# Normalising half the tiles of each layer norm on GpSimd instead of all of them on VectorE

## The chip, the cores and the metric

The kernel runs on one core of one Trainium2 chip, in one launch. The metric is the device time of that launch in microseconds (us), taken as the median of several runs; lower is better. The core's engines are TensorE (PE, with its weight loads shown apart as PEld), VectorE (DVE), ScalarE (ACT), GpSimd (POOL) and SyncE (SP, which here only issues DMAs). Each runs its own list of instructions in order, and they wait for one another through semaphores.

## The reference, cut to what matters

The model is a stack of eight residual blocks on an activation of 16 x 256 x 128 float32 values. Every block first normalises its input row by row, without gain or bias:

```python
def _layernorm(x, axis=-1, eps=1e-05):
    m = jnp.mean(x, axis=axis, keepdims=True)
    v = jnp.var(x, axis=axis, keepdims=True)
    return (x - m) / jnp.sqrt(v + eps)
...
x = x + _L0_attn_a_ref(_layernorm(x, axis=-1), ...)
x = x + _L0_ffn_ref(_layernorm(x, axis=-1), ...)
x = x + _L0_attn_b_ref(_layernorm(x, axis=-1), ...)
x = x + _L0_ffn_ref(_layernorm(x, axis=-1), ...)
x = x + _L1_attn_a_ref(_layernorm(x, axis=-1), ...)
x = x + _L1_ffn_ref(_layernorm(x, axis=-1), ...)
x = x + _L1_attn_b_ref(_layernorm(x, axis=-1), ...)
x = x + _L1_ffn_ref(_layernorm(x, axis=-1), ...)
```

So there are eight layer norms (n1 to n8 in the kernel), each over 4096 rows of 128 values. What the blocks compute behind them is not touched.

## The kernel before, in words

The activation lives in the on-chip tile `X` for the whole launch: 128 partitions, 32 tiles of 128 rows, 128 float32 values per row. `XN` holds the normalised rows in the same layout, and `XNT` the same with rows and columns exchanged, which is what the matmuls of the next block read. The program is a chain of phases. Each ends in a clearing of its semaphores and a barrier of all engines (`Phase.__exit__`, lines 81 to 87), so nothing of one phase runs beside another.

`layernorm` (from line 237) is such a phase and is called eight times:

- VectorE takes the statistics of the 32 tiles (`tile_statistics`, L230) and turns them into one mean and one reciprocal deviation per row (`row_statistics`, L208 to L221, with the square root on ScalarE in between, L262).
- VectorE then normalises the 32 tiles one by one (L255), each in one instruction that subtracts the mean and multiplies by the reciprocal deviation. Both are columns of one value per partition. After every fourth tile it raises the semaphore `normed`.
- TensorE waits for `normed`, then turns the four tiles of the group by a multiplication with the identity (L273) into one PSUM bank of four, and raises `turn`.
- ScalarE waits for `turn` and copies the bank of 512 columns to `XNT` (L265), which raises `evac`. TensorE needs `evac` of the group four earlier before it writes to a bank again.

GpSimd has no work in this phase. The loop over the eight groups that sets the order on VectorE is this:

```python
for g in range(G):
    for t in range(4 * g, 4 * g + 4):
        ins = nc.vector.tensor_scalar(sh.XN[:, t, :], sh.X[:, t, :], mean[:, t:t + 1], rstd[:, t:t + 1],
                                      ALU.subtract, ALU.mult)
    ins.then_inc(normed, 1)
```

`row_statistics` is also called by `top2_mixture` (a mixture of experts that ends in a layer norm of its own, twice in the program); there too VectorE alone uses what it returns. Two other places serve the prediction as measurements only: `routing_constants` (L137 to L168), where GpSimd fills tiles while VectorE copies one, and a stage of `delta_attention` (L1963 to L2011) with the same kind of turned tiles.

Of the kernel before, what the change touches and what calls it, by code (L numbers as in the profile page):

```python
# [15 lines left out]
ALU = mybir.AluOpType  # L16
# [17 lines left out]
def reached(eng, sem, count):  # L34

    if not isinstance(count, int) or count > 0:
        eng.wait_ge(sem, count)
# [163 lines left out]
                pool.wait_ge(made, 3)  # L201


def row_statistics(nc, dve, st, mean, rstd, work, chain, sqrt_in, sqrt_done):

    even, odd = (st[:, :, 1], st[:, :, 2]), (st[:, :, 4], st[:, :, 5])
    a, b, c = work[:, 0, :], work[:, 1, :], work[:, 2, :]
    nc.vector.tensor_tensor(a, even[0], odd[0], ALU.add).then_inc(chain, 1)  # L208
    nc.vector.tensor_tensor(b, even[0], odd[0], ALU.subtract).then_inc(chain, 1)
    nc.vector.tensor_tensor(c, even[1], odd[1], ALU.add).then_inc(chain, 1)  # L210
    dve.wait_ge(chain, 3)
    nc.vector.tensor_scalar(mean[:], a, 0.5, None, ALU.mult).then_inc(chain, 1)
    nc.vector.scalar_tensor_tensor(out=work[:, 3, :], in0=b, scalar=0.25, in1=b, op0=ALU.mult,
                                   op1=ALU.mult).then_inc(chain, 1)
    dve.wait_ge(chain, 5)
    nc.vector.scalar_tensor_tensor(out=work[:, 4, :], in0=c, scalar=1.0 / P, in1=work[:, 3, :], op0=ALU.mult,
                                   op1=ALU.add).then_inc(chain, 1)
    dve.wait_ge(chain, 6)
    nc.vector.tensor_scalar(work[:, 5, :], work[:, 4, :], 1e-5, None, ALU.add).then_inc(sqrt_in, 1)
    dve.wait_ge(sqrt_done, 1)  # L220
    nc.vector.reciprocal(rstd[:], work[:, 6, :]).then_inc(chain, 1)  # L221
    dve.wait_ge(chain, 7)


def tile_statistics(nc, dve, st, src, stats):

    with dve.Fori(0, TILES // 8) as m:
        for i in range(8):
            t = 8 * m + i
            nc.vector.bn_stats(st[:, bass.ds(t, 1), :].rearrange("p a s -> p (a s)"),  # L230
                               src[:, bass.ds(t, 1), :].rearrange("p a c -> p (a c)")).then_inc(stats, 1)
    dve.wait_ge(stats, TILES)


def layernorm(nc, sh, name):

    G = TILES // 4
    with Phase(nc, name) as ph:
        st, mean, rstd, work = ph.sb("st", [P, TILES, 6]), ph.sb("mean", [P, TILES]), ph.sb("rstd", [P, TILES]), \
            ph.sb("work", [P, 7, TILES])
        turned = ph.bank("turned", (P, 4, 512))
        stats, chain, sqrt_in, sqrt_done = ph.sem("stats"), ph.sem("chain"), ph.sem("sqrt_in"), ph.sem("sqrt_done")
        normed, turn, evac = ph.sem("normed"), ph.sem("turn"), ph.sem("evac")
        with nc.Block() as block:
            @block.vector
            def _(dve):  # L250
                tile_statistics(nc, dve, st, sh.X, stats)
                row_statistics(nc, dve, st, mean, rstd, work, chain, sqrt_in, sqrt_done)
                for g in range(G):
                    for t in range(4 * g, 4 * g + 4):
                        ins = nc.vector.tensor_scalar(sh.XN[:, t, :], sh.X[:, t, :], mean[:, t:t + 1], rstd[:, t:t + 1],  # L255
                                                      ALU.subtract, ALU.mult)
                    ins.then_inc(normed, 1)

            @block.scalar
            def _(act):  # L260
                act.wait_ge(sqrt_in, 1)
                nc.scalar.activation(work[:, 6, :], work[:, 5, :], ACT.Sqrt).then_inc(sqrt_done, 1)  # L262
                for g in range(G):
                    act.wait_ge(turn, g + 1)
                    nc.scalar.activation(sh.XNT[:, g * 512:(g + 1) * 512], turned[:, g % 4, :], ACT.Copy).then_inc(evac, 1)  # L265

            @block.tensor
            def _(pe):
                for g in range(G):
                    pe.wait_ge(normed, g + 1)  # L270
                    reached(pe, evac, g - 3)
                    for i in range(4):
                        ins = nc.tensor.transpose(turned[:, g % 4, i * P:(i + 1) * P], sh.XN[:, 4 * g + i, :], sh.ident[:])  # L273
                    ins.then_inc(turn, 1)
# [549 lines left out]
def top2_mixture(nc, sh, name, Wg, bg, W1, b1, W2, b2, gamma, beta):  # L824
# [8 lines left out]
    with Phase(nc, name) as ph:  # L833
# [17 lines left out]
             "b2_mm", "b2_ok", "up_mm", "hid_ok", "down_mm", "acc_ok"))  # L851
        st, mean, rstd, work = ph.sb("st", [P, TILES, 6]), ph.sb("mean", [P, TILES]), ph.sb("rstd", [P, TILES]), \
            ph.sb("work", [P, 7, TILES])
        stats, chain2, sqrt_in, sqrt_done, centred, shifted, summed = (ph.sem(x) for x in (
            "stats", "chain2", "sqrt_in", "sqrt_done", "centred", "shifted", "summed"))

        def two_chunks(n, first):

# [2 lines left out]
        with nc.Block() as block:  # L861
            @block.sync
            def _(sp):
                sp.dma_start(wg[:], Wg).then_inc(wl, 16)
                sp.dma_start(bgb[:], bg.partition_broadcast(P)).then_inc(wl, 16)
                sp.dma_start(b2s[:], b2).then_inc(wl, 16)
                sp.dma_start(w1[:], W1.rearrange("e d f -> d e f")).then_inc(loaded, 16)
                sp.dma_start(w2[:], W2.rearrange("e (j f) d -> f e j d", j=2)).then_inc(loaded, 16)
                with nc.allow_non_contiguous_dma("the biases are a few thousand values"):
                    sp.dma_start(b1s[:], b1.rearrange("e (j f) -> f e j", j=2)).then_inc(loaded, 16)  # L870
                sp.dma_start(gam[:], gamma.partition_broadcast(P)).then_inc(loaded, 16)
                sp.dma_start(bet[:], beta.partition_broadcast(P)).then_inc(loaded, 16)
# [162 lines left out]
        with nc.Block() as block:  # L1035
            @block.vector
            def _(dve):
                dve.wait_ge(stats, TILES)
                row_statistics(nc, dve, st, mean, rstd, work, chain2, sqrt_in, sqrt_done)
                with dve.Fori(0, TILES // 8) as m:  # L1040
                    for i in range(8):

                        t = 8 * m + i
                        a, x = (buf[:, bass.ds(t, 1), :].rearrange("p a c -> p (a c)") for buf in (acc, sh.X))
                        nc.vector.scalar_tensor_tensor(out=a, in0=a, scalar=mean[:, bass.ds(t, 1)], in1=gam[:],
                                                       op0=ALU.subtract, op1=ALU.mult).then_inc(centred, 1)
                    for i in range(8):
                        t = 8 * m + i
                        a, x = (buf[:, bass.ds(t, 1), :].rearrange("p a c -> p (a c)") for buf in (acc, sh.X))
                        dve.wait_ge(centred, t + 1)  # L1050
                        nc.vector.scalar_tensor_tensor(out=x, in0=a, scalar=rstd[:, bass.ds(t, 1)], in1=x,
                                                       op0=ALU.mult, op1=ALU.add).then_inc(summed, 1)

            @block.scalar
            def _(act):
                act.wait_ge(sqrt_in, 1)
                nc.scalar.activation(work[:, 6, :], work[:, 5, :], ACT.Sqrt).then_inc(sqrt_done, 1)
# [1191 lines left out]
```

## Time and profile before

| | us |
|---|---|
| median of 3 runs | 4605.37 (4603.25 to 4612.34) |
| the profiled execution | 4600.9 |
| its span in the trace | 4599.1 |
| first normalising instruction to last copy to `XNT`, sum over the eight layer norms | 77.11 |
| VectorE's share of that in L255 | 66.33 |

The 1.8 us between the profiled execution and its span lie outside the traced instructions. Busy time is the time in which an engine ran an instruction, and a share of the whole span is a mean over very different phases, so the layer norms have to be read in windows of their own. The duration of one instruction is longer than the distance from one start to the next on the same engine, as an engine starts the next before the last has quite ended; where instructions follow each other closely, the distance is the price.

### The profile page before, as it was taken

Reading aid. Unit: us, or ns where it says so; the run is one execution under the profiler, and the core shown is the slowest. Engines: PE = TensorE matmul, PEld = TensorE weight load, DVE = VectorE, ACT = ScalarE, POOL = GpSimd, SP = SyncE. Lnnn points to the kernel's source line nnn. Section 1 sums busy time; section 2 is a strip of 40 time slices with the busy share of each in tenths; the row PEclk is TensorE's granted clock in tenths of the full one; section 3 lists DMA queues with packets and bytes.
Section 4 is the critical chain, followed back from the end, with each engine's and each line's share of the span. In section 5 each row is a group of like instructions: output and inputs, shape, how many; then the busy total and the mean of one; then the engine's idle time right before and its main releaser. Section 6 shows DMA issues by size and latency. Waiting matters only on the chain. (4 is left out here: it accounts for less than half of the span.)

```text
span 4599.1 us, 93352 instructions
## 1 busy us (share of the span) xinstructions
PE 3851.2 (84%) x24738; PEld 3022.9 (66%) x24738; DVE 3002.7 (65%) x9151; ACT 2152.0 (47%) x6005; POOL 1073.1 (23%) x2042
## 2 busy tenths in 40 slices
PE   7999999999889699999988968999999386433267
PEld 5888888888767466666656746888888264322145
DVE  5666666666633566666663345999999245899954
ACT  4555555555523344444442324777777133211123
POOL 1222222222200000000000002333333132466633
PEclk9999999999989899999998989999999588766678
DMA  0000000000000000000000000000000411000003
GB/s 23 4 3 1 4 4 3 1 4 4 0 20 0 3 3 2 2 2 2 4 1 20 0 4 5 6 6 6 6 6 5 76 47 37 1 1 1 1 14 87
DMA packets 79403, 48.07 MB, mean 10 GB/s; under 512 B 20928, under 2 KB 73936, under 8 KB 79280
## 3 DMA queue, kind: packets, MB, share of 16 engines
q1 hardware_dynamic: 74736, 37.40, 3.7%
q0 software_dynamic: 4544, 9.35, 0.6%
q8 instruction: 39, 0.64, 0.1%
q14 instruction: 84, 0.69, 0.1%
HBM read 25.94 MB, written 16.59 MB: 9 GB/s over the span
## 5 line engine op out<-in xcount | busy, mean ns | idle before, releaser
L346 POOL TENSOR_TENSOR aa_prob<-aa_prob,aa_inv 128x128 f32<-128x128 f32 (+1 forms) x512 | 248.5, 506 | 919.1 <-DVE aa_inv L562 914.6
L369 PE MATMUL aa_proj<-aa_xs,aa_w 128*128 128x256 f32 x1280 | 362.5, 398 | 12.4 <-DMA aa_w<-in_L_attn_a_W_qkv 10.9
L753 ACT ACTIVATE ab_prob<-ab_ps_score,ab_low 128x128 f32<-128x128 f32 (+1 forms) x512 | 211.0, 422 | 328.4 <-DVE ab_low L786 328.4
L477 ACT ACTIVATE aa_qkv<-aa_proj 128x512 f32<-128x512 f32 x384 | 229.3, 597 | 258.7 <-PE aa_proj L369 198.1
L1712 ACT ACTIVATE lm_prob<-lm_ps_score,lm_low 128x256 f32<-128x256 f32 x512 | 236.7, 471 | 157.2 <-DVE lm_low L1786 85.3
L1662 PEld LDWEIGHTS lm_ps_out<-la_v,lm_probT 128*128 128x128 f32 x2048 | 253.3, 192 | 73.5 <-issue 65.9
L2050 PE MATMUL dr_bank<-da_rT,da_spread 128*128 (+1 forms) x256 | 96.5, 466 | 244.1 <-ACT dr_RW L2068 237.1
L648 POOL COPY ab_xs<-ab_latT 128x256 f32 (+1 forms) x128 | 51.2, 400 | 1032.6 <-PE ab_proj L665 724.7
L1641 PE MATMUL lm_ps_score<-lm_unit 128*128 128x256 f32 x1024 | 270.2, 387 | 5.5 <-DVE lm_unit L1776 5.5
L1662 PE MATMUL lm_ps_out<-la_v,lm_probT 128*128 (+1 forms) x2048 | 257.5, 252 | 19.4 <-issue 16.3
L369 PEld LDWEIGHTS aa_proj<-aa_xs,aa_w 128*128 128x128 f32 x1280 | 214.1, 191 | 44.7 <-issue 12.7
L1604 POOL TENSOR_TENSOR lm_sq<-lm_comp 128x512 f32<-128x512 f32 x128 | 133.4, 1042 | 465.7 <-DVE lm_comp L1753 465.7
L535 DVE SCALAR_TENSOR_TENSOR aa_look<-aa_th_look,aa_ahead 128x384 f32<-128x384 f32 x256 | 183.1, 715 | 88.5 <-ACT aa_th_look L483 88.5
L488 ACT ACTIVATE aa_th_su<-aa_look_su 128x384 f32<-128x384 f32 x256 | 125.5, 490 | 242.8 <-PE aa_look_su L413 242.8
L2100 POOL TENSOR_TENSOR dr_toward<-dr_S,XN 128x64 f32<-128x64 f32 x512 | 181.0, 372 | 217.6 <-DVE dr_S L2129 154.4
L2050 PEld LDWEIGHTS dr_bank<-da_rT,da_spread 128*128 128x128 f32 x256 | 59.2, 238 | 259.4 <-issue 249.5
L494 ACT ACTIVATE aa_prob<-aa_minus,aa_low 128x128 f32<-128x128 f32 (+1 forms) x512 | 225.5, 444 | 0.9 <-DVE aa_low L554 0.9
L1768 DVE RECIPROCAL lm_inv_n<-lm_norm 128x256 f32<-128x256 f32 x128 | 223.1, 1743 | 0.1
L542 DVE SCALAR_TENSOR_TENSOR aa_gated<-aa_th_su,aa_look_su 128x384 f32<-128x384 f32 x256 | 142.0, 555 | 108.5 <-ACT aa_th_su L488 106.9
L273 PE MATMUL n_turned<-ident,XN 128*128 128x128 f32 x256 | 55.7, 370 | 181.7 <-DVE XN L255 181.5
L1776 DVE TENSOR_TENSOR lm_unit<-lm_comp,lm_inv_n 64x512 f32<-64x512 f32 x256 | 201.9, 789 | 7.4
L786 DVE TENSOR_REDUCE ab_low<-ab_ps_score 128x1 f32<-128x128 f32 (+1 forms) x512 | 158.3, 351 | 65.5 <-PE ab_ps_score L677 65.5
(435 smaller groups left out, 10803.4 us busy)
## 6 DMA issues: line engine op xcount, KB each, us to landing
rt_slots<-rc_empty SPq DMA_DIRECT2D x2, 2515.5 KB, 26.2
lm_unit<-la_qk SPq DMA_DIRECT2D x256, 16.0 KB
XN<-rt_back SPq DMA_DIRECT2D x8, 512.0 KB, 6.2
aa_w<-in_L_attn_a_W_qkv SPq DMA_DIRECT2D x8, 384.0 KB, 3.4
out<-X SPq DMA_DIRECT2D x1, 2048.0 KB, 8.7
fc_xin<-rt_slots SPq DMA_DIRECT2D x1, 1483.5 KB, 10.4
fd_xin<-rt_slots SPq DMA_DIRECT2D x1, 1483.5 KB, 10.1
fa_w<-in_L_ffn_W SPq DMA_DIRECT2D x1, 1024.0 KB, 5.4
```

The source lines that it names most:

```text
L346: ins = nc.gpsimd.tensor_tensor(prob[:, h, a:b], prob[:, h, a:b], inv[:, h, t:t + 1].broadcast_to([P, b - a]), ALU.mult)
L369: ins = nc.tensor.matmul(proj[:, i * SEQ:(i + 1) * SEQ], w[:, m, :], xs[:, k, :], start=True, stop=True)
L477: nc.scalar.activation(qkv[:, k, j, :, :].rearrange("p a b -> p (a b)"), proj[:], ACT.Copy, scale=SCALE if j == 0 else 1.0).then_inc(kept, 1)
L494: nc.scalar.activation(prob[:, h, a:b], minus[:, h, a:b], ACT.Exp, bias=low[:, h, t:t + 1], scale=-1.0, accum_out=total[:, h, t:t + 1]).th ...
L535: nc.vector.scalar_tensor_tensor(out=look[:, h, :], in0=th_look[:, h, :], scalar=1.0, in1=ahead[:], op0=ALU.add, op1=ALU.mult).then_inc(lo ...
L753: nc.scalar.activation(prob[:, h, a:b], ps_score[:, h, a:b], ACT.Exp, bias=low[:, h, t:t + 1], accum_out=total[:, h, t:t + 1]).then_inc(ex ...
L1641: ins = nc.tensor.matmul(ps_score[:, h, c * SEQ:(c + 1) * SEQ], unit[:, j, i, h, 0, c, :], unit[:, j, i, h, 1, :, :], start=True, stop=True)
L1662: ins = nc.tensor.matmul(ps_out[:, i, (2 * h + s) * HD:(2 * h + s + 1) * HD], probT[:, h, t, s * P:(s + 1) * P], v[:, bass.ds((n % BATCH) ...
L1712: nc.scalar.activation(prob[:, h, s, :], ps_score[:, h, s * SEQ:(s + 1) * SEQ], ACT.Exp, bias=low[:, h, s:s + 1], accum_out=totals[:, i, h ...
L1768: nc.vector.reciprocal(inv_n[:, j, i], norm[:, j, i]).then_inc(inv_ok, 1)
L1776: ins = nc.vector.tensor_tensor(unit[rows, j, i, h], comp[rows, j, i], inv_n[rows, j, i].unsqueeze(2).broadcast_to([64, 2, 2, HALF]), ALU. ...
L2100: nc.gpsimd.tensor_tensor(toward[:, :, part], S[:, :, part], WV[:, half, :, part, j], ALU.add).then_inc(toward_ok, 1)
```

## The change

In `layernorm`, VectorE now normalises the first two tiles of each group of four and GpSimd the last two, with the same operation and operands. GpSimd starts when VectorE has written the reciprocal deviations, told by a new semaphore `known`, and raises a second new semaphore, `normed_too`, after each pair. TensorE waits for both `normed` and `normed_too` before it turns a group. In `row_statistics` the last step raises `known` instead of the seventh count of `chain`, so `top2_mixture` gets a semaphore of that name as well and is otherwise as before.

```diff
-def row_statistics(nc, dve, st, mean, rstd, work, chain, sqrt_in, sqrt_done):
+def row_statistics(nc, dve, st, mean, rstd, work, chain, sqrt_in, sqrt_done, known):
...
-    nc.vector.reciprocal(rstd[:], work[:, 6, :]).then_inc(chain, 1)
-    dve.wait_ge(chain, 7)
+    nc.vector.reciprocal(rstd[:], work[:, 6, :]).then_inc(known, 1)
+    dve.wait_ge(known, 1)
...
                 for g in range(G):
-                    for t in range(4 * g, 4 * g + 4):
+                    for t in range(4 * g, 4 * g + 2):
                         ins = nc.vector.tensor_scalar(sh.XN[:, t, :], sh.X[:, t, :], mean[:, t:t + 1], rstd[:, t:t + 1],
                                                       ALU.subtract, ALU.mult)
                     ins.then_inc(normed, 1)
+
+            @block.gpsimd
+            def _(pool):
+                pool.wait_ge(known, 1)
+                for g in range(G):
+                    for t in range(4 * g + 2, 4 * g + 4):
+                        ins = nc.gpsimd.tensor_scalar(sh.XN[:, t, :], sh.X[:, t, :], mean[:, t:t + 1], rstd[:, t:t + 1],
+                                                      ALU.subtract, ALU.mult)
+                    ins.then_inc(normed_too, 1)
...
                 for g in range(G):
                     pe.wait_ge(normed, g + 1)
+                    pe.wait_ge(normed_too, g + 1)
                     reached(pe, evac, g - 3)
```

GpSimd's list from the end of the loading phase (L183) through the first layer norm into the first block, before; `ISA` rows are the clearing of semaphores at a phase's end (L86) or, at L346, a setting that stands ahead of GpSimd's first use of a kind of instruction:

```order
L183 UNCONDITIONAL_BRANCH [waits ld_made]
L86 ISA [waits barrier_Pool_Activation_PE_DVE_SP_gather] x2
L324 UNCONDITIONAL_BRANCH [waits barrier_Pool_Activation_PE_DVE_SP_gather]
L326 MEMSET aa_causal 128x384
L327 MEMSET aa_ahead 128x384
L328 MEMSET aa_bar 128x128
```

The same stretch of GpSimd in the changed kernel (its lines below the edit are 11 higher):

```order
L183 UNCONDITIONAL_BRANCH [waits ld_made]
L86 ISA [waits barrier_Pool_Activation_PE_DVE_SP_gather]
L260 UNCONDITIONAL_BRANCH [waits barrier_Pool_Activation_PE_DVE_SP_gather]
L265 ISA
L265 TENSOR_SCALAR XN<-X,n_mean,n_rstd 128x128 [waits n1_known]
L265 TENSOR_SCALAR XN<-X,n_mean,n_rstd 128x128 x15
L249 UNCONDITIONAL_BRANCH
L86 ISA [waits barrier_Pool_Activation_PE_DVE_SP_gather]
L335 UNCONDITIONAL_BRANCH [waits barrier_Pool_Activation_PE_DVE_SP_gather]
L337 MEMSET aa_causal 128x384
L338 MEMSET aa_ahead 128x384
```

Sixteen normalising instructions have come in between the two barriers, with one wait ahead of the first; the setting now stands at L265, ahead of that wait, in the first layer norm alone, and is gone from the first block. The other seven layer norms get the sixteen instructions without it.

TensorE's list at the start of the first layer norm, before:

```order
L267 UNCONDITIONAL_BRANCH [waits barrier_Pool_Activation_PE_DVE_SP_release]
L273 MATMUL n_turned<-ident,XN 128x128 [waits n1_normed]
L273 MATMUL n_turned<-ident,XN 128x128 x3
L273 MATMUL n_turned<-ident,XN 128x128 [waits n1_normed]
L273 MATMUL n_turned<-ident,XN 128x128 x3
```

And in the changed kernel:

```order
L277 UNCONDITIONAL_BRANCH [waits barrier_Pool_Activation_PE_DVE_SP_release]
L284 MATMUL n_turned<-ident,XN 128x128 [waits n1_normed_too,n1_normed]
L284 MATMUL n_turned<-ident,XN 128x128 x3
L284 MATMUL n_turned<-ident,XN 128x128 [waits n1_normed_too,n1_normed]
L284 MATMUL n_turned<-ident,XN 128x128 x3
```

TensorE's instructions stand in the same order; each group's first one has one wait more.

## Rows read from the trace of the kernel before

**Rows 1.** The page: span, and the turning of the layer norms in its costliest groups.

```profile
span 4599.1 us, 93352 instructions
...
L273 PE MATMUL n_turned<-ident,XN 128*128 128x128 f32 x256 | 55.7, 370 | 181.7 <-DVE XN L255 181.5
```

**Rows 2.** Windows, one per layer norm, first L255 to last L265; last number pair DMA.

```profile
core 0: us, PE busy (x) PEld busy (x) DVE busy (x) ACT busy (x) POOL busy (x), PEclk, DMA share, GB/s
...
1261.85:1271.50 9.65, 6.53 (x32) 4.41 (x32) 8.30 (x32) 4.78 (x8) 0.00 (x0) 0.76 0.00 0
1580.58:1590.22 9.64, 7.30 (x32) 5.04 (x32) 8.29 (x32) 4.78 (x8) 0.00 (x0) 0.65 0.00 0
...
sum 77.11, PE 55.67 PEld 38.02 DVE 66.33 ACT 38.22 POOL 0.00; mean PE 6.96 PEld 4.75 DVE 8.29 ACT 4.78 POOL 0.00
```

**Rows 3.** Timeline of the first layer norm: start, us, engine, line, what, idle before.

```profile
22.01 0.35 DVE L221 RECIPROCAL n_rstd<-n_work 128x32 f32<-128x32 f32 x1 [0.29 <-ACT n_work L262]
22.40 8.29 DVE L255 TENSOR_SCALAR XN<-X,n_mean,n_rstd 128x128 f32<-128x128 f32 x32
23.57 0.72 PEld L273 LDWEIGHTS n_turned<-ident,XN 128*128 128x128 f32 x4 [23.57 <-DVE XN L255]
...
27.67 0.42 PEld L273 LDWEIGHTS n_turned<-ident,XN 128*128 128x128 f32 x4 [0.31 <-DVE XN L255]
27.71 1.26 ACT L265 ACTIVATE XNT<-n_turned 128x512 f32<-128x512 f32 x2 [0.33 <-PE n_turned L273]
...
30.75 0.66 PE L273 MATMUL n_turned<-ident,XN 128*128 128x128 f32 x4 [0.36 <-DVE XN L255]
31.44 0.60 ACT L265 ACTIVATE XNT<-n_turned 128x512 f32<-128x512 f32 x1 [0.42 <-PE n_turned L273]
...
32.74 0.42 POOL L326 MEMSET aa_causal<- 128x384 f32 x1 [30.43 <-POOLq L87]
```

**Rows 4.** Windows inside the third layer norm, and of L1963: same columns as rows 2.

```profile
1581.75:1587.30 5.55, 5.55 (x22) 4.00 (x23) 5.55 (x23) 2.69 (x5) 0.00 (x0) 0.50 0.00 0
1587.30:1590.22 2.92, 1.75 (x12) 1.03 (x10) 1.57 (x7) 2.09 (x4) 0.00 (x0) 0.99 0.00 0
3919.55:3926.65 7.10, 6.98 (x32) 5.40 (x32) 7.10 (x8) 4.18 (x7) 0.00 (x0) 0.58 0.00 0
```

**Rows 5.** Timeline of L1963: the same turning with its input ready earlier.

```profile
3918.74 4.91 DVE L2011 TENSOR_TENSOR XN<-XN,ds_inv 128x512 f32<-128x512 f32 x8
3919.55 1.57 PEld L1963 LDWEIGHTS ds_bank<-ident,XN 128*128 128x128 f32 x8 [7.63 <-issue]
...
3925.99 0.42 PEld L1963 LDWEIGHTS ds_bank<-ident,XN 128*128 128x128 f32 x4 [0.29 <-issue]
```

**Rows 6.** Groups by line and shape on POOL: count, busy us, mean ns, idle before.

```profile
L346 POOL TENSOR_TENSOR aa_prob<-aa_prob,aa_inv 128x256 f32<-128x256 f32 x256 | 157.1, 614 | 0.0
...
L346 POOL TENSOR_TENSOR aa_prob<-aa_prob,aa_inv 128x128 f32<-128x128 f32 x256 | 102.1, 399 | 919.1 <-DVE aa_inv L562 914.6
...
L333 POOL TENSOR_SCALAR_AFFINE_SELECT aa_ahead<-aa_ahead 128x128 f32<-128x128 f32 x2 | 0.6, 290 | 0.0
```

**Rows 7.** Timeline of POOL in the first block: starts of instructions that follow each other.

```profile
33.73 0.29 POOL L331 TENSOR_SCALAR_AFFINE_SELECT aa_causal<-aa_causal 128x128 f32<-128x128 f32 x1
33.98 0.29 POOL L333 TENSOR_SCALAR_AFFINE_SELECT aa_ahead<-aa_ahead 128x128 f32<-128x128 f32 x1
...
54.21 0.97 POOL L346 TENSOR_TENSOR aa_prob<-aa_prob,aa_inv 128x128 f32<-128x128 f32 x2 [18.51 <-DVE aa_inv L562]
```

**Rows 8.** Groups by line and shape on DVE.

```profile
L1762 DVE TENSOR_SCALAR lm_n<-lm_n 128x512 f32<-128x512 f32 x64 | 27.9, 436 | 5.7 <-POOL lm_n L1607 3.8
...
L2011 DVE TENSOR_TENSOR XN<-XN,ds_inv 128x512 f32<-128x512 f32 x8 | 4.9, 686 | 0.0
...
L208 DVE TENSOR_TENSOR n_work<-n_st 128x32 f32<-128x32 f32 x8 | 1.7, 215 | 0.3
...
L212 DVE TENSOR_SCALAR n_mean<-n_work 128x32 f32<-128x32 f32 x8 | 1.4, 181 | 0.3
```

**Rows 9.** Timeline of the routing constants: POOL fills while DVE copies.

```profile
3605.14 4.29 POOL L137 MEMSET rc_empty<- 128x5031 f32 x1 [21.42 <-POOLq L87]
...
3605.61 4.40 DVE L168 COPY rt_earlier<-rt_same 128x256 f32<-128x256 f32 x2
3609.37 0.20 POOL L138 MEMSET rt_ones<- 128x128 f32 x1
3609.52 0.34 POOL L139 MEMSET rt_before<- 128x128 f32 x1
```

**Rows 10.** The instructions of L168: shortest, median and longest in ns, first and last start.

```profile
L168 DVE COPY rt_earlier<-rt_same x2: 367/2239/4111, 3605.6 to 3609.6; 128x256 f32<-128x256 f32 x2
```

More of the change, by code:

```diff
@@ L246, in layernorm @@
         stats, chain, sqrt_in, sqrt_done = ph.sem("stats"), ph.sem("chain"), ph.sem("sqrt_in"), ph.sem("sqrt_done")
-        normed, turn, evac = ph.sem("normed"), ph.sem("turn"), ph.sem("evac")
+        normed, normed_too, turn, evac = ph.sem("normed"), ph.sem("normed_too"), ph.sem("turn"), ph.sem("evac")
+        known = ph.sem("known")
         with nc.Block() as block:
@@ L251, in _ @@
                 tile_statistics(nc, dve, st, sh.X, stats)
-                row_statistics(nc, dve, st, mean, rstd, work, chain, sqrt_in, sqrt_done)
+                row_statistics(nc, dve, st, mean, rstd, work, chain, sqrt_in, sqrt_done, known)
                 for g in range(G):
-                    for t in range(4 * g, 4 * g + 4):
+                    for t in range(4 * g, 4 * g + 2):
                         ins = nc.vector.tensor_scalar(sh.XN[:, t, :], sh.X[:, t, :], mean[:, t:t + 1], rstd[:, t:t + 1],
@@ L853, in top2_mixture @@
             ph.sb("work", [P, 7, TILES])
-        stats, chain2, sqrt_in, sqrt_done, centred, shifted, summed = (ph.sem(x) for x in (
-            "stats", "chain2", "sqrt_in", "sqrt_done", "centred", "shifted", "summed"))
+        stats, chain2, sqrt_in, sqrt_done, known, centred, shifted, summed = (ph.sem(x) for x in (
+            "stats", "chain2", "sqrt_in", "sqrt_done", "known", "centred", "shifted", "summed"))
         def two_chunks(n, first):
@@ L1038, in _ @@
                 dve.wait_ge(stats, TILES)
-                row_statistics(nc, dve, st, mean, rstd, work, chain2, sqrt_in, sqrt_done)
+                row_statistics(nc, dve, st, mean, rstd, work, chain2, sqrt_in, sqrt_done, known)
                 with dve.Fori(0, TILES // 8) as m:
```

## The prediction, as it was made before the changed kernel was run

> **What bounds the kernel now.** I read the page for the size of the stage, then windows on each layer norm, then the timeline inside one, then rows elsewhere for prices that a layer norm does not show.
>
> The page says that TensorE's turning of normalised tiles sits idle for 181.7 us in all, nearly all of it until VectorE's normalising [rows 1]. Part of that is the earlier wait for the statistics, so the windows decide: from the first normalising instruction to the last copy into `XNT` each of the eight layer norms takes 9.63 to 9.65 us, 77.11 us in sum, of which VectorE is busy 66.33 us; ScalarE and TensorE are busy less and GpSimd not at all [rows 2]. No DMA takes part. So at the most 77 us of 4600 are in play, and barriers on both sides hand any gain there straight on to the end.
>
> The timeline shows the shape. VectorE's 32 instructions take 8.29 us from 22.40 [rows 3]. With 0.35 us for the last one, the distance between starts is (8.29 - 0.35) / 31 = 0.256 us, and a group of four takes 1.025 us. The first turning starts at 23.58 (its weight load at 23.57), 1.18 us behind the first normalising; the last turning starts at 30.75, seven groups later; the last copy ends at 32.04 [rows 3]. So 9.64 = 1.18 + 7 x 1.025 + 1.29. Every group's turning waits for VectorE: this is the wait that the change attacks.
>
> What comes next is TensorE's own pace. The granted clock is at its lower level (0.50 of full, 1.2 GHz) in the first 5.55 us of turning in the third layer norm and 0.99 after that [rows 4]; there TensorE is busy in all of the 5.55 us. What a group costs at the lower level when its input is ready is shown by the same turning in L1963, granted 0.58 on average [rows 4]: the first weight load at 3919.55, the eighth group's at 3925.99, so 6.44 / 7 = 0.92 us per group [rows 5]. At the full level ScalarE's copies bound it: two in 1.26 us, and 0.60 for one, so 0.66 us per group [rows 3].
>
> **The change, term by term.** Per layer norm, VectorE loses 16 of 32 instructions and needs 0.51 us per group; it is no longer the bound. GpSimd gains 16. TensorE's groups start with one more wait. The `known` signal replaces a count of `chain` on the same instruction: nothing. The setting ahead of GpSimd's first use moves from the first block to the first layer norm, ahead of the wait there, with VectorE's statistics beside it (GpSimd idle for the 30.43 us before 32.74 [rows 3]); I cost it at nothing, and if uncovered it would be paid once, not eight times. No DMA and no queue other than GpSimd's and TensorE's is passed. Behind GpSimd's instructions only the barrier is queued, and ScalarE ends after it. In `top2_mixture` only a semaphore's name changes: nothing.
>
> The disputed price is GpSimd's distance P from one normalising instruction to the next; the trace has no such instruction on GpSimd. From below: the affine select, one 128x128 tile in and one out, starts at 33.73 and 33.98, so 0.25 us apart [rows 7]. From above: subtract and multiply as two separate instructions, each a multiply of a tile with a one-column operand as in L346. Two of those, 128x128 and 128x256, together take 0.97 us, the second 0.614 [rows 6, 7], so the first costs 0.97 - 0.61 = 0.36 us, and two 0.72. The nearest row is this L346 instruction: tile and column in, one operation. Its column is streamed as a second input, which costs 0.36 - 0.25 = 0.11 us over the affine select. The new instruction has two columns; I take them as fetched once rather than streamed, at half of that extra above L346: P = 0.36 + 0.05 = 0.41 us.
>
> To this comes a collision. VectorE's `tensor_scalar` from on-chip memory to on-chip memory runs at 0.51 ns per element, (427 to 436 - 181) ns over 480 elements, where two-input instructions need (686 - 215) / 480 = 0.98 [rows 8]. So it moves two elements per step, and such instructions do exclude GpSimd's: in the routing constants a VectorE copy issued at 3605.61 took 4.11 us instead of the second one's 0.37, because GpSimd's 4.29 us fill, begun at 3605.14, ran until 3609.43; and once both engines had work, GpSimd's fill of 128x128 grew from 0.20 to 0.34 us [rows 9, 10]. The loser waits, but the added 0.14 us is far less than the copy's own 0.37: it is about the time in which 256 elements stream at that rate (256 x 0.51 ns = 0.13 us). For 128 elements this is 0.07 us, in every 0.256 us of VectorE's work, so a random start of GpSimd's meets it 3 times in 10. I charge 0.03 us on average: P = 0.44.
>
> The Trainium skill ("SBUF — State Buffer", section "Who interferes with whom") has the rule that speaks against this change: VectorE in a two-port mode, which `tensor_scalar` can enter, and GpSimd lock each other out for a whole instruction. The trace agrees that they exclude each other; that the whole listed duration is locked is not what the 0.14 us shows. By the whole duration the sum would come out as in the first rival below.
>
> The sum per layer norm, from VectorE's first instruction: GpSimd starts at about 0.05 (VectorE itself starts 0.04 after the 0.35 us reciprocal begun at 22.01 [rows 3]); its pair is ready at 0.05 + 0.44 + 0.48 = 0.97, and TensorE starts 0.07 later, as it does now: 1.04, not 1.18. At full speed from then on, TensorE would take 0.92 us per group until the clock rises. The mean clock of a window tells when: 0.76 means (1 - 0.76) x 2 x 9.65 = 4.6 us at the lower level, 0.65 means 6.7 [rows 2]; the eight average near 5.8. So some 5.1 of the seven steps cost 0.92 and 1.9 cost 0.66, and TensorE would reach its last group at 1.04 + 4.7 + 1.25 = 7.0. GpSimd's last pair lets it start at 0.05 + 15 x 0.44 + 0.48 + 0.07 = 7.20, so that is later and decides. With the same 1.29 behind: 8.49 us instead of 9.64, **1.15 us less, 9.2 us less in eight**. The profiled execution of 4600.9 us (span 4599.1 [rows 1]) would take 4591.7. It lies 4.5 us below the median of the runs, so I forecast 4605.4 - 9.2 = **4596 us**.
>
> Both ends of the unknown: with P = 0.25 and no collision TensorE starts at 0.66 and bounds the whole: 0.66 + 5.1 + 1.0 + 1.29 = 8.0, a gain of 1.63 x 8 = 13 us. With 0.72 + 0.03: 0.05 + 15 x 0.75 + 0.79 + 0.07 + 1.29 = 13.45, a loss of 30 us. Break-even is 16 P = 8.2, P = 0.51.
>
> **The rivals.** (a) *GpSimd and VectorE exclude each other for whole instructions.* Place: the two halves of each group, while both run. Each GpSimd instruction then also waits out one of VectorE's, P = 0.256 + 0.41 = 0.67; 0.05 + 15 x 0.67 + 0.71 + 0.07 + 1.29 = 12.2, so 2.5 x 8 = 20 us slower: 4625. It decides from 0.10 us of added wait on. For it: the exclusion itself [rows 9, 10]. Against: the 0.14 us there, with instructions that streamed twice as much. (b) *GpSimd's instruction is simply slow*, P over 0.55 with two streamed columns or two passes: 5 to 30 us slower, 4610 to 4635. For it: the columns double the stream in L346. Against: nothing but L346's own price for one. (c) *GpSimd takes VectorE's place as the bound at about the old pace*, P of 0.46 to 0.55: within 8 us of 4605. (d) *GpSimd is as fast as on an affine select*, P below 0.40, TensorE and its clock become the bound: 11 to 13 us faster, 4593. The Trainium skill ("GPSIMD Engine Reference", section 4.1) puts one-input operations on GpSimd at roughly line rate, which is this rival; the affine select's 0.25 us is as near as the trace comes to it.
>
> **How the numbers follow.** I give (a) 0.12, (b) 0.11, (c) 0.23, (d) 0.24 and the forecast, P of 0.40 to 0.46 and a gain of 8 to 11 us, 0.30. A difference of 0.2% (9.2 us) is about what a measurement of this kernel can tell from no change, and the forecast stands right on it: of its 0.30 I count 0.18 as faster and 0.12 as the same. Faster is then 0.24 + 0.18 = 0.42; the same 0.23 + 0.12 = 0.35; slower 0.23. The range runs from 4590 (a gain of 13 us, and 2 us of the runs' scatter) to 4618, which takes in the nearer part of (b) and leaves the farther part and (a) out, some 0.16, with perhaps 0.03 below. Within forecast, (c) and (d) alone it would be 4590 to 4612.
>
> **What would show it.** In the timeline of the changed kernel's layer norms: GpSimd's 16 normalising instructions 0.40 to 0.46 us apart; VectorE's 16 done in 4 to 6 us instead of 8.29, some of them stretched by collisions; the first turning about 1.04 us behind; groups 0.9 us apart; the window from first normalising to last copy 8.4 to 8.6 us. The wait behind most of TensorE's idle time would change from VectorE to GpSimd. I am wrong if GpSimd's distance is above 0.51 us, and if so the length of VectorE's instructions tells (a) from (b): in (a) they stretch and GpSimd speeds up once VectorE is done; in (b) GpSimd's distance stays long to the end. If layer norms shrink as said and the whole does not, the clock granted to the following blocks would have shifted.

## The result: slower, and the profile after

The changed kernel took 4655.59 us in the median of 4 runs (4652.22 to 4659.75), the kernel before beside it 4604.31 us (4591.02 to 4612.34): a ratio of 1.0115, 95% interval 1.0089 to 1.0140. Timed again later on another occasion, the ratio was 1.0093, interval 1.0070 to 1.0116. The forecast was 4596 us, a gain; the measured time lies far above the range of 4590 to 4618.

The profiled execution took 4656.85 us. On the page, the span and the groups that answer to [rows 1]; GpSimd's normalising is new, and TensorE's turning idles 206.8 us where it idled 181.7:

```profile
span 4655.1 us, 93384 instructions
...
L265 POOL TENSOR_SCALAR XN<-X,n_mean,n_rstd 128x128 f32<-128x128 f32 x128 | 102.3, 815 | 755.3 <-DVE n_rstd L221 755.3
...
L284 PE MATMUL n_turned<-ident,XN 128*128 128x128 f32 x256 | 69.6, 427 | 206.8 <-DVE XN L256 158.5
```

The windows of the second and third layer norm and the sum over all eight, which answer to [rows 2] (same columns):

```profile
1268.54:1283.19 14.65, 8.69 (x32) 5.72 (x32) 4.46 (x16) 4.78 (x8) 12.76 (x16) 0.50 0.00 1
1601.34:1616.00 14.66, 8.70 (x32) 5.72 (x32) 4.46 (x16) 4.78 (x8) 12.77 (x16) 0.50 0.00 0
...
sum 117.38, PE 69.58 PEld 45.78 DVE 35.74 ACT 38.24 POOL 102.27; mean PE 8.70 PEld 5.72 DVE 4.47 ACT 4.78 POOL 12.78
```

VectorE's busy time fell from 8.29 to 4.47 us per layer norm as the edit intends, but GpSimd needs 12.78 us for its half, and the window grew from 9.64 to 14.65 us. The eight grew from 77.11 to 117.38 us: 40.3 us. The clock granted to TensorE now stays at 0.50 (1.2 GHz) to the end of the window in the second to the eighth layer norm, where it rose before. (The first one's row reads 1.00, but its groups of four turnings take the same 1.09 us as in the others.)

The timeline of the second layer norm (start, us, engine, line, what, idle before):

```profile
1268.15 0.35 DVE L221 RECIPROCAL n_rstd<-n_work 128x32 f32<-128x32 f32 x1 [0.30 <-ACT n_work L272]
1268.54 4.46 DVE L256 TENSOR_SCALAR XN<-X,n_mean,n_rstd 128x128 f32<-128x128 f32 x16
1268.61 8.09 POOL L265 TENSOR_SCALAR XN<-X,n_mean,n_rstd 128x128 f32<-128x128 f32 x10 [17.91 <-DVE n_rstd L221]
...
1270.43 1.08 PE L284 MATMUL n_turned<-ident,XN 128*128 128x128 f32 x4 [13.85 <-DVE XN L256]
...
1275.29 1.09 PE L284 MATMUL n_turned<-ident,XN 128*128 128x128 f32 x4 [0.47 <-POOL XN L265]
...
1281.47 1.09 PE L284 MATMUL n_turned<-ident,XN 128*128 128x128 f32 x4 [0.47 <-issue]
1282.60 0.60 ACT L275 ACTIVATE XNT<-n_turned 128x512 f32<-128x512 f32 x1 [0.96 <-PE n_turned L284]
```

GpSimd starts 0.07 us behind VectorE, so the new wait itself is cheap. Then VectorE finishes all sixteen tiles in 4.46 us while GpSimd has done five. Its first ten instructions in 8.09 us are 0.81 us apart, and the last six take (12.76 - 8.09) / 6 = 0.78 us each; over the whole window 12.76 us for sixteen with 0.80 for the last is (12.76 - 0.80) / 15 = 0.797 us. The forecast had 0.44. In this view the wait that ends later is sometimes put down to VectorE, which had long been done; it is GpSimd's.

Both engines' normalising instructions, by line (shortest, median, longest in ns):

```profile
L265 POOL TENSOR_SCALAR XN<-X,n_mean,n_rstd x128: 789/801/987, 22.8 to 4471.3; 128x128 f32<-128x128 f32 x128
...
L256 DVE TENSOR_SCALAR XN<-X,n_mean,n_rstd x128: 331/389/446, 22.7 to 4463.4; 128x128 f32<-128x128 f32 x128
```

VectorE's stretched from a median of 346 to 389 ns, and 4.46 us for sixteen puts them 0.275 us apart instead of 0.256. So both engines slow each other, and by little. What remains of the difference between the two profiled executions, 56.0 us of span less 40.3, lies in the blocks: 9.1 us in the mixture behind the second layer norm and 10.3 in that behind the fourth, less in the others and partly of the other sign. That remainder had to be explained as well.

### The profile page after: what moved, and what is told of

It is laid out like the page before. It is cut to its first block and busy times, and to the rows that moved or that the text cites. A ratio compares the mean times of both kernels' runs of the same rounds, so it can differ in the third digit from the quotient of the medians.

```text
span 4655.1 us, 93384 instructions
## 1 busy us (share of the span) xinstructions
PE 3884.0 (83%) x24738; PEld 3041.5 (65%) x24738; DVE 2972.3 (64%) x9023; ACT 2154.5 (46%) x6005; POOL 1178.3 (25%) x2170
## 5 line engine op out<-in xcount | busy, mean ns | idle before, releaser
L380 PE MATMUL aa_proj<-aa_xs,aa_w 128*128 128x256 f32 x1280 | 362.3, 398 | 12.1 <-DMA aa_w<-in_L_attn_a_W_qkv 10.8
L265 POOL TENSOR_SCALAR XN<-X,n_mean,n_rstd 128x128 f32<-128x128 f32 x128 | 102.3, 815 | 755.3 <-DVE n_rstd L221 755.3
L284 PE MATMUL n_turned<-ident,XN 128*128 128x128 f32 x256 | 69.6, 427 | 206.8 <-DVE XN L256 158.5
```

The costliest lines, as they stand in the source:

```text
L380: ins = nc.tensor.matmul(proj[:, i * SEQ:(i + 1) * SEQ], w[:, m, :], xs[:, k, :], start=True, stop=True)
```

## The experiments

**Second profiles of both kernels, unchanged.** The question was whether the mixtures lose time because of the change.

> The kernel before, profiled a second time. The question is the 15 us that the changed kernel loses outside its layer norms, of which 9.1 and 10.3 us lie in the two mixtures behind the second and fourth layer norm (from the last copy to XNT to the next layer norm's first statistics: 298.8 and 296.8 us before, 307.9 and 307.0 after). Theory 'the slow layer norm does it': the two bodies repeat within 1 us, 298 and 297. Theory 'chance of one execution' (TensorE's granted clock goes up and down in the mixtures' first 90 us, and where it does so falls differently in every execution): they differ by several us from 298.8 and 296.8.

> The changed kernel, profiled a second time. Theory 'the slow layer norm does it': both mixtures' bodies again 307 to 308 us. Theory 'chance of one execution': they differ by several us from 307.9 and 307.0, and one may come near 297. The layer norms themselves, first normalising instruction to last copy, repeat at 14.65 us in either.

Measured: 4612.1 us for the kernel before (median of the runs beside it 4611.88) and 4653.73 for the changed one, whose layer norms again took 14.63 to 14.65 us, the first 14.79. Windows of the two mixtures, from the last copy to `XNT` to the next layer norm's statistics, in the first profile of the kernel before:

```profile
1271.50:1570.32 298.82, 259.87 (x1440) 191.75 (x1440) 113.57 (x388) 95.26 (x140) 10.70 (x16) 0.91 0.03 8
2421.51:2718.27 296.76, 258.48 (x1440) 190.55 (x1440) 113.68 (x388) 95.24 (x141) 10.89 (x16) 0.92 0.03 8
```

In its second profile:

```profile
1272.66:1569.30 296.64, 257.53 (x1440) 189.65 (x1440) 113.62 (x387) 95.23 (x140) 10.70 (x16) 0.92 0.03 8
2419.90:2724.58 304.68, 265.63 (x1440) 195.55 (x1440) 113.78 (x388) 95.23 (x140) 10.70 (x16) 0.89 0.03 8
```

And in the first profile of the changed kernel:

```profile
1283.19:1591.07 307.88, 268.43 (x1440) 197.47 (x1440) 113.70 (x387) 95.27 (x141) 10.90 (x16) 0.88 0.03 8
2451.70:2758.72 307.02, 268.53 (x1440) 197.03 (x1440) 113.61 (x388) 95.28 (x141) 10.71 (x16) 0.88 0.03 8
```

The reader is to compare the third-last number: the same 1440 matmuls take 297 us at a mean granted clock of 0.92 and 308 at 0.88. The kernel before shows 296.8 and 304.7 us for one and the same mixture in two executions, so part of this is chance. The changed kernel repeated 307.8 and 307.2, which still left the other theory open.

**GpSimd's price, form by form.** The changed kernel with another GpSimd instruction in several layer norms:

```diff
-                        ins = nc.gpsimd.tensor_scalar(sh.XN[:, t, :], sh.X[:, t, :], mean[:, t:t + 1], rstd[:, t:t + 1],
-                                                      ALU.subtract, ALU.mult)
+                        xn, x, m, r = sh.XN[:, t, :], sh.X[:, t, :], mean[:, t:t + 1], rstd[:, t:t + 1]
+                        if name == "n2":
+                            ins = nc.gpsimd.tensor_scalar(xn, x, 0.0, 1.0, ALU.subtract, ALU.mult)
+                        elif name == "n3":
+                            ins = nc.gpsimd.tensor_scalar(xn, x, r, None, ALU.mult)
...
+                if name == "n6":
+                    dve.wait_ge(normed_too, G)
```

> A measurement of GpSimd's price, not a version: the changed kernel, whose layer norms give GpSimd different instructions. First and eighth: as changed (0.80 to 0.84 us apart). Second: constants 0 and 1 in place of the two columns (so its half of the tiles is not normalised). Third: one operation with one column (the mean is left out). Fourth: both columns, but only the first 64 values of each row (the others are left as they were). Fifth: one instruction over the 256 values of two tiles, with one tile's columns. Sixth: as changed, but VectorE begins only when GpSimd is done. Seventh: one operation with a constant (a copy). Theory 'mutual exclusion with VectorE': the sixth falls to about 0.41 us, as forecast. Theory 'the columns are dear': the sixth stays at 0.80; second and seventh fall to about 0.3 to 0.4; third to about 0.55 to 0.6; fourth 0.70 or more; fifth 0.91. Theory 'it is slow per value': the sixth 0.80, the second also about 0.80; the fourth near 0.5, the fifth near 1.4. Theory 'the second operation is dear': third and seventh fall alike, to about 0.4, and the second stays.

Measured, groups by line and shape on GpSimd (count, busy us, mean ns, idle before):

```profile
L283 POOL TENSOR_SCALAR XN<-X,n_mean,n_rstd 128x128 f32<-128x128 f32 x48 | 38.0, 805 | 96.0 <-DVE n_rstd L221 96.0
...
L277 POOL TENSOR_SCALAR XN<-X,n_mean,n_rstd 128x256 f32<-128x256 f32 x8 | 10.2, 1283 | 295.1 <-DVE n_rstd L221 295.1
...
L273 POOL TENSOR_SCALAR XN<-X,n_mean,n_rstd 128x64 f32<-128x64 f32 x16 | 9.9, 649 | 33.0 <-DVE n_rstd L221 33.0
L269 POOL TENSOR_SCALAR XN<-X 128x128 f32<-128x128 f32 x16 | 9.8, 642 | 17.7 <-DVE n_rstd L221 17.7
L271 POOL TENSOR_SCALAR XN<-X,n_rstd 128x128 f32<-128x128 f32 x16 | 9.4, 603 | 293.4 <-DVE n_rstd L221 293.4
...
L281 POOL TENSOR_SCALAR XN<-X 128x128 f32<-128x128 f32 x16 | 8.1, 531 | 23.7 <-DVE n_rstd L221 23.7
```

And the sixth layer norm's GpSimd work, with VectorE held back until it is done:

```profile
3704.10 12.41 POOL L283 TENSOR_SCALAR XN<-X,n_mean,n_rstd 128x128 f32<-128x128 f32 x16 [62.37 <-DVE n_rstd L221]
```

Without VectorE the sixteen still take 12.41 us, (12.41 - 0.79) / 15 = 0.775 us apart instead of 0.797: mutual exclusion costs 0.02 us per instruction over all sixteen, and that theory, which expected 0.41 without VectorE, falls. The 0.02 is an average: VectorE is at work during about the first six, so the 12.76 - 12.41 = 0.35 us fall on those, some 0.05 to 0.06 us each. The price, by durations, is about additive. One operation with a constant takes 0.531 us, one with a column 0.603: 0.07 per column. Two operations with constants take 0.642: 0.11 for the second. Together 0.53 + 0.11 + 2 x 0.07 = 0.78, against 0.805 for the full form in the midst of VectorE's work. And it grows with the width: from 64 values (0.65 us) over 128 (0.81) to 256 (1.28) the last step is (1283 - 805) / 128 = 3.7 ns per value; the shortest of each, which VectorE does not stretch, are 572, 787 and 1212 ns, and give (787 - 572) / 64 = 3.4 and (1212 - 787) / 128 = 3.3. So of the 0.79 us some 0.42 are per value and 0.15 for the columns. "Slow per value" came nearest; columns and the second operation add to it. (The two-constant form at 0.642 is a miss of that theory, which had it at 0.80.)

**Other instructions for the same work.**

```diff
+                        if name == "n1":
+                            nc.gpsimd.tensor_tensor(xn, x, m.broadcast_to([P, P]), ALU.subtract).then_inc(first, 1)
...
+                        elif name == "n7":
+                            ins = nc.gpsimd.tensor_copy(xn, x)
...
+                    if name == "n1":
+                        pool.wait_ge(first, 2 * (g + 1))
+                        for t in range(4 * g + 2, 4 * g + 4):
+                            ins = nc.gpsimd.tensor_tensor(sh.XN[:, t, :], sh.XN[:, t, :],
+                                                          rstd[:, t:t + 1].broadcast_to([P, P]), ALU.mult)
```

> Again a measurement of prices, the changed kernel with other GpSimd instructions in some layer norms. First: subtract and multiply as two tensor_tensor instructions, each with a column spread over the tile. Third and fifth: one operation with a constant over 64 and over 256 values (parts left unnormalised), to go with the 0.52 us over 128. Seventh: a plain copy of 128 values (not normalised). The others as changed. By additive prices (0.52 for one operation with a constant over 128 values, 0.12 for the second operation, 0.075 for each column) and 3.3 us per 1000 values in the two-column form: third 0.35, fifth 0.85 to 0.95. First: 0.36 + 0.36 = 0.72 per tile by the rows of the kernel before, a little cheaper than the one instruction. Seventh: 0.24 to 0.29, as the copies elsewhere. If the first is 0.80 or more, the price lies in reading a column and not in this kind of instruction.

Measured, the same view:

```profile
L273 POOL TENSOR_SCALAR XN<-X 128x256 f32<-128x256 f32 x8 | 6.7, 868 | 297.4 <-DVE n_rstd L221 297.4
L267 POOL TENSOR_TENSOR XN<-X,n_mean 128x128 f32<-128x128 f32 x16 | 6.1, 403 | 20.1 <-DVE n_rstd L221 20.1
L283 POOL TENSOR_TENSOR XN<-XN,n_rstd 128x128 f32<-128x128 f32 x16 | 6.1, 401 | 0.6
L269 POOL TENSOR_SCALAR XN<-X 128x64 f32<-128x64 f32 x16 | 5.4, 410 | 294.0 <-DVE n_rstd L221 294.0
L277 POOL COPY XN<-X 128x128 f32<-128x128 f32 x16 | 4.1, 308 | 23.9 <-DVE n_rstd L221 23.9
```

And the start of the first layer norm, on GpSimd and on VectorE:

```profile
22.41 0.76 POOL L267 TENSOR_TENSOR XN<-X,n_mean 128x128 f32<-128x128 f32 x2 [20.09 <-DVE n_rstd L221]
23.24 0.76 POOL L283 TENSOR_TENSOR XN<-XN,n_rstd 128x128 f32<-128x128 f32 x2
23.96 0.76 POOL L267 TENSOR_TENSOR XN<-X,n_mean 128x128 f32<-128x128 f32 x2
...
22.36 6.38 DVE L256 TENSOR_SCALAR XN<-X,n_mean,n_rstd 128x128 f32<-128x128 f32 x16
```

Subtract and multiply as two `tensor_tensor` instructions have durations of 0.403 + 0.401 us, as much as the one `tensor_scalar`. From start to start, the price that the prediction uses, two of them in 0.76 us with 0.40 for the last are 0.36 us apart, so the pair costs 0.72 us, as I had expected; with the wait for the first half, two tiles take 23.96 - 22.41 = 1.55 us, 0.775 each, just the 0.775 of the `tensor_scalar` alone. So on GpSimd the fused instruction saves nothing. A pair at 0.80 or more was to show that the price lies in reading a column; 0.72 does not show it. The copy takes 0.308 us and the one-operation `tensor_scalar` over the same 128 values, with no column, 0.531, so it is this kind of instruction that is dear, at (868 - 531) / 128 = 2.6 ns per value, and not the reading of a tile. For 64 values I had expected 0.35; they took 0.41 beside VectorE. VectorE's own sixteen stretched more here: 6.38 us, about 0.40 us apart instead of 0.256, so how much GpSimd slows VectorE depends on GpSimd's instruction.

These two kernels also test the schedule behind the forecast, since they run the same layer norm at several prices. Three windows, from first normalising to last copy: in the first price kernel its seventh (0.50 us apart) and third (0.58),

```profile
3906.35:3915.84 9.49, 6.33 (x32) 4.37 (x32) 4.29 (x16) 4.78 (x8) 8.07 (x16) 0.76 0.01 2
1596.44:1607.24 10.80, 7.32 (x32) 4.84 (x32) 4.65 (x16) 4.77 (x8) 9.37 (x16) 0.67 0.00 0
```

and in the second one the copies (0.25 us apart):

```profile
3906.04:3912.97 6.93, 5.38 (x32) 5.14 (x32) 4.24 (x16) 4.35 (x8) 4.11 (x16) 0.70 0.01 2
```

In this last one TensorE no longer waits for GpSimd, and ScalarE's copies show the pace of its groups:

```profile
3907.90 0.60 ACT L293 ACTIVATE XNT<-n_turned 128x512 f32<-128x512 f32 x1 [2.28 <-PE n_turned L302]
3908.76 0.60 ACT L293 ACTIVATE XNT<-n_turned 128x512 f32<-128x512 f32 x1 [0.26 <-PE n_turned L302]
...
3910.42 2.55 ACT L293 ACTIVATE XNT<-n_turned 128x512 f32<-128x512 f32 x5 [0.21 <-PE n_turned L302]
```

The first copies stand 0.86 us apart (granted clock 0.53 up to 3910.42), the last five (2.55 - 0.60) / 4 = 0.49 us (clock 1.00).

**Slow layer norms without GpSimd.** The kernel before, with two extra VectorE instructions per group:

```diff
+                    for i in range(2):
+                        nc.vector.tensor_scalar(spare[:, 2 * g + i, :], sh.X[:, 4 * g, :], mean[:, 4 * g:4 * g + 1],
+                                                rstd[:, 4 * g:4 * g + 1], ALU.subtract, ALU.mult)
```

> The kernel before, GpSimd idle in the layer norms, but VectorE normalises the first tile of each group twice more into a spare tile, so that a group takes 6 x 0.256 = 1.54 us, about GpSimd's pace in the changed kernel. Layer norms: 13.8 to 14.2 us each, 33 to 37 us more in eight. Theory 'GpSimd's work has an effect of its own behind the layer norms': the mixtures behind the second and fourth layer norm scatter as in the kernel before (297 to 305 us), and the whole is 33 to 37 us above the kernel before of the same chip. Theory 'a slow layer norm leaves TensorE's clock low': both mixtures at 307 to 308, the whole 45 to 52 us above. Theory 'the mixtures depend on where their start falls between the clock's steps, by chance in each execution': the runs scatter over some 20 us and the profile shows any of 297 to 308.

Measured: ratio 1.0080 (1.0061 to 1.0100), 4643.61 us against 4606.79, so 37 us more. Its second layer norm and its two mixtures:

```profile
1268.03:1282.23 14.20, 8.92 (x32) 5.72 (x32) 12.39 (x48) 4.78 (x8) 0.00 (x0) 0.50 0.00 0
1282.23:1591.98 309.75, 272.25 (x1440) 199.02 (x1440) 112.36 (x387) 95.28 (x141) 10.70 (x16) 0.87 0.03 8
2451.89:2759.68 307.79, 268.33 (x1440) 197.42 (x1440) 113.69 (x387) 95.28 (x141) 10.71 (x16) 0.88 0.03 8
```

All eight layer norms took 14.2 us, 8 x (14.20 - 9.64) = 36.5 us more, which accounts for the whole difference between the medians. A layer norm at this pace costs about the same whichever engine is slow. The slow mixtures speak for the second theory, the 37 us against it; the two did not decide between the last two theories.

**The changed kernel, timed again.**

> The changed kernel, timed again beside the others. Theory 'chance': twelve runs scatter as widely as the kernel before, some 20 to 35 us, with a low end near 4637 (both mixtures at 297). Theory 'a slow layer norm leaves the clock low': they stay within some 10 us of 4655, and the profile shows both mixtures at 307 to 308 a third time.

Measured: 4642.75 us, six runs from 4627.85 to 4660.70; ratio 1.0093 (1.0070 to 1.0116). The profiled one was the fastest. Its layer norms were as slow as ever (14.61 us, the first 14.76), and its mixtures:

```profile
1282.15:1579.94 297.79, 259.07 (x1440) 191.06 (x1440) 113.16 (x387) 95.22 (x140) 10.71 (x16) 0.91 0.03 8
2440.63:2738.32 297.69, 257.33 (x1440) 190.25 (x1440) 114.38 (x387) 95.27 (x140) 10.87 (x16) 0.92 0.03 8
```

So the changed kernel has fast mixtures too: a slow layer norm does not force the slow ones, though its clock was at 0.50 to the end of the layer norm here as well. Whether it makes them likelier is another question, to which the account below returns. The first four timed runs had all lain within 8 us and looked like a property of the kernel.

**TensorE kept busy within the layer norms.**

```diff
+                    if g < G - 1:
+                        for i in range(3):
+                            nc.tensor.transpose(idle[:, ((3 * g + i) // 4) % 4, ((3 * g + i) % 4) * P:((3 * g + i) % 4 + 1) * P],
+                                                sh.ident[:], sh.ident[:])
```

> The changed kernel with three more transposes of the identity into an idle PSUM bank behind each of the first seven groups, so that TensorE does not pause between groups. (They compute nothing that is used.) Layer norms still follow GpSimd: 14.2 to 14.9 us, and TensorE's clock should rise within them. Theory 'a slow layer norm leaves the clock low': the mixtures return to 297 and the whole is 10 to 20 us below the changed kernel. Theory 'chance, or where the start falls between the clock's steps': the whole within 8 us of the changed kernel and the mixtures anywhere from 297 to 308.

Measured: ratio 1.0087 (1.0067 to 1.0108), 4647.46 us against 4642.75 for the changed kernel beside it. The second layer norm and the two mixtures:

```profile
1267.84:1282.00 14.16, 8.71 (x53) 6.87 (x53) 4.46 (x16) 4.78 (x8) 12.72 (x16) 0.82 0.00 1
1282.00:1583.18 301.18, 262.34 (x1440) 193.37 (x1440) 113.40 (x388) 95.24 (x140) 10.89 (x16) 0.90 0.03 8
2446.73:2754.45 307.72, 267.28 (x1440) 196.75 (x1440) 114.24 (x387) 95.25 (x141) 11.07 (x16) 0.88 0.03 8
```

The layer norms fell by 0.5 us each, to 14.15 to 14.17 (the first 14.31): with the clock raised inside them, their last turning and copy are shorter. The mixtures took 301.2 and 307.7 us. So a raised clock in the layer norm does not bring the fast mixtures back, and the low one of the run above did not prevent them: the clock left by the layer norm does not decide them by itself.

**Three tiles to VectorE, one to GpSimd.** The version that the prices point to: 0.80 to 0.84 us for one tile on GpSimd beside three on VectorE.

```diff
-                    for t in range(4 * g, 4 * g + 2):
+                    for t in range(4 * g, 4 * g + 3):
...
-                    for t in range(4 * g + 2, 4 * g + 4):
+                    for t in range(4 * g + 3, 4 * g + 4):
```

> VectorE normalises three tiles of each group, GpSimd the fourth. At GpSimd's 0.80 to 0.84 us per instruction its pace is one group per 0.84 us, VectorE's 3 x 0.27 = 0.81, TensorE's 0.92 at the lower clock: theory 'only the instruction's price was wrong' expects each layer norm at 8.4 to 8.8 us from first normalising to last copy instead of 9.64, 7 to 10 us less in eight, and 4595 to 4598 us in all; the mixtures behind them as before. Theory 'GpSimd in the layer norm costs the later blocks 15 us whatever its pace': layer norms as said, but the whole 4610 or more. Theory 'exclusion grows with VectorE's share' (VectorE is now at it all the time): GpSimd at 1.0 us or more per instruction and no gain in the layer norms.

Measured: 4591.29 us, twelve runs from 4584.74 to 4605.65, against 4611.88 for the kernel before beside it: ratio 0.9962, interval 0.9944 to 0.9980. Its layer norms:

```profile
1261.79:1269.90 8.11, 6.08 (x32) 5.12 (x32) 6.76 (x24) 4.67 (x8) 6.62 (x8) 0.69 0.00 0
1587.63:1595.93 8.30, 6.54 (x32) 6.06 (x32) 6.78 (x24) 4.67 (x8) 6.63 (x8) 0.58 0.00 0
...
sum 65.36, PE 49.77 PEld 42.52 DVE 54.03 ACT 37.37 POOL 53.20; mean PE 6.22 PEld 5.32 DVE 6.75 ACT 4.67 POOL 6.65
```

VectorE and GpSimd are busy 6.75 and 6.65 us: the two shares are now balanced. GpSimd's instructions are (6.62 - 0.80) / 7 = 0.83 us apart with VectorE at work all the time, so exclusion does not grow with VectorE's share; and the whole, below the kernel before, rules out a loss of 15 us in the later blocks whenever GpSimd works in the layer norms. The layer norms came out shorter than the 8.4 to 8.8 us expected, which had counted 0.92 us per group for TensorE; it needs 0.86, as the layer norm with the copies shows. The eight windows sum to 65.36 us, 11.75 less than before [rows 2]. That is 0.25% of the whole, within the interval of 0.20% to 0.56%; its two mixtures took 307.5 and 296.9 us, and what the rest of the 20 us between the medians is beyond scatter was not settled.

## Why the prediction was wrong

**The step that failed is the price of GpSimd's instruction.** I put P, the distance from one to the next, at 0.41 us, by adding half of a stream's extra to the one-operation `tensor_tensor` of L346 [rows 6, 7]; it is 0.775 us alone and 0.797 in the changed kernel. The columns were sized well: 0.11 + 0.05 = 0.16 us over the affine select in P, 0.15 measured (whether they are fetched once or per value was not measured). But the assumption under that, that the instruction otherwise costs what an affine select or a copy does, was false: one operation with a constant, no column at all, is 0.50 us from start to start against the affine select's 0.25, and the second operation, which P counts at nothing, adds 0.11. With these two, 0.41 + 0.25 + 0.11 = 0.77. The bound from above, two separate `tensor_tensor` instructions at 0.72 us, with 0.03 for collisions 0.75, was the row nearest to the truth. I took it for an end and left it out of the range.

**The schedule around it was right where GpSimd sets the pace.** The forecast's own formula is 0.05 + 15 P + (P + 0.04) + 0.07 + 1.29 = 1.45 + 16 P. The windows give, at P = 0.50, 9.49 us (formula 9.5); at 0.58, 10.80 (10.8 with 0.585); and at 0.797 the formula has 14.20 where 14.65 was measured. Of the missing 0.45, 0.43 is the last turning and copy at TensorE's lower clock: the changed kernel's last group starts at 1281.47 and ends at 1283.19, 1.72 us, where the formula has 1.29. That TensorE, waiting in every group, would not see its clock rise at all was missing from the forecast. Break-even at P = 0.51 holds, too: at 0.50 the window is 9.49 against 9.64 before. TensorE's own pace, which would have bounded a faster GpSimd, was sized too long: 0.92 and 0.66 us per group in the forecast, 0.86 and 0.49 in the layer norm with the copies. The error had no part in this result, where GpSimd decides.

**The rivals.** (b), a GpSimd instruction that is simply slow, is what happened, at more than its upper price of 0.75; it had 0.11. Its reasons, the columns or a second pass, are only part of it: 0.15 us for both columns and 0.11 for the second operation, on a base of 0.53. (a), exclusion for whole instructions, did not: beside VectorE a GpSimd instruction takes some 0.05 us longer, where (a) needs 0.256. The sign I gave for telling them apart held in the main: in the changed kernel GpSimd's distance stays long after VectorE is done (0.78 us). VectorE's instructions did stretch, which I had named as a sign of (a), so that sign by itself would have misled. The 0.03 us charged for collisions was about right, and VectorE's stretch cost nothing here. In "SBUF — State Buffer", section "Who interferes with whom", the Trainium skill has the loser blocked for the other's whole instruction. Some 0.05 us on GpSimd's side and 0.02 on VectorE's, against listed durations of 0.39 and 0.80, is far less than that; the stretch on both sides does show that they interfere. (d), a GpSimd as fast as on an affine select, would have held for a copy (0.25 us apart, and then a layer norm of 6.93 us, shorter than the 8.0 I had given that case) but not for `tensor_scalar`, at 2.6 ns per value for one operation. In "GPSIMD Engine Reference", section 4.1, the Trainium skill has one-input operations at "roughly line-rate". The 2.6 ns per value measured here, against 0.51 for VectorE's `tensor_scalar` [rows 8], does not agree with that.

**The terms costed at nothing** were nothing: GpSimd started 0.07 us behind VectorE, also in the first layer norm with its setting, and the statistics in the mixtures' own layer norms, from L208 to the start of L221, took 1.52 us before and 1.52 to 1.53 after. The scatter of the blocks behind, 10 us per mixture, was not in the forecast at all; it does not decide the verdict, as the layer norms' 40.3 us alone are 0.88% of 4604 us. The second timing's interval (0.70% to 1.16%) holds that; the first one's begins just above, at 0.89%, and both mixtures were slow in the one of its runs that was profiled. Whether slow layer norms make slow mixtures likelier stays open. In all ten profiles, 11 of the 14 mixtures behind a layer norm of over 11 us took over 307 us, and one of the six behind a layer norm of under 10 us. The whole times show no clear cost of it: beyond what the layer norms explain, the medians of the changed kernel (twice), the slowed VectorE and the busy TensorE lie between 4 us below and 11 us above the kernel before.

## What to carry to other kernels

A price for an instruction on another engine is taken from the same kind of instruction there, or else from the dearest way to put it together out of rows that exist: here two `tensor_tensor` at 0.36 us each, 0.72 together, would have come within a tenth of the price of the fused `tensor_scalar`, which on GpSimd costs three times VectorE's (0.797 against 0.256 us). When work is split over two engines of different speed, split it by the ratio of the prices (three to one here), since a group waits for the slower half. And where one block scatters by 10 us from execution to execution, two profiles can't be compared in sum: compare the windows that the change touches.

## What was not expected of the hardware

GpSimd's `tensor_scalar` on 128 partitions of float32 needs 2.6 ns per value for one operation and 3.3 to 3.4 for two, a column 0.07 us; by durations, its `tensor_tensor` with a column spread over the tile needs 0.40 us for 128 values, where the one-operation `tensor_scalar` with a column needs 0.60. VectorE's normalising, 0.256 us apart alone, is 0.275 apart beside GpSimd's `tensor_scalar` and about 0.40 beside its `tensor_tensor`. The two mixtures run the same 1440 matmuls in 297 or in up to 310 us at mean granted clocks of 0.92 to 0.88, in either kernel; what picks one or the other in an execution stayed open.
